# Second attention: a new order of units and banks, and score banks handed over one by one

## The reference, cut to what matters

```python
h = x                                      # [4, 512, 128]
q, k, v = h @ Wq, h @ Wk, h @ Wv           # 16 heads of 8 channels
q, k = rope(q), rope(k)                    # the angle depends on the sequence's number alone
s = (q @ k.T) * 8 ** -0.5                  # per sequence and head: 512 x 512, no mask
x = layernorm(x + softmax(s) @ v)          # this x is also kept: the final stage adds it again
```

## Time and profile before

| | us |
|---|---|
| three runs, median (lowest to highest) | 1745.11 (1740.25 to 1749.67) |
| the profiled execution | 1740.4 |
| its span, first to last instruction | 1737.5 |
| mean granted TensorE clock | 0.946 of full speed |

### The profile page before, as it was taken

One profiled execution on the slowest core, in us unless ns is written; L12 is line 12 of the kernel. 1 busy time (PEld: TensorE's weight loads), 2 busy tenths in 40 slices (PEclk: granted clock), 3 DMA queues, 4 the chain that ended last, 5 costly groups with the idle time before them and its releaser, 6 DMA issues. The chain is left out here.

```text
span 1737.5 us, 30440 instructions
## 1 busy us (share of the span) xinstructions
PE 1533.2 (88%) x10286; PEld 1045.5 (60%) x10286; DVE 1139.0 (66%) x2214; ACT 1077.1 (62%) x2354; POOL 512.3 (29%) x474
## 2 busy tenths in 40 slices
PE   6999999999799999999788888868899877999975
PEld 4777777777578888888533232224666544666643
DVE  2666666766577777777666667746777543676735
ACT  2655555555478888888546666655777633777741
POOL 0222222222321212222100000016666413767611
PEclk9999999999889999999968899988999987999988
DMA  7000000000012221122000000000000000000000
GB/s 225 2 2 0 0 0 0 0 0 1 1 64 74 73 73 69 65 72 73 1 1 1 1 1 1 1 1 1 2 1 2 2 0 1 1 2 1 1 1 24
DMA packets 18976, 36.35 MB, mean 21 GB/s; under 512 B 5748, under 2 KB 10992, under 8 KB 16688
## 3 DMA queue, kind: packets, MB, share of 16 engines
q1 hardware_dynamic: 18880, 35.09, 6.0%
HBM read 33.91 MB, written 1.18 MB: 20 GB/s over the span
## 5 line engine op out<-in xcount | busy, mean ns | idle before, releaser
L968 DVE TENSOR_TENSOR m_hidp<-m_hid,m_hidp 128x512 fp32r<-128x512 f32 x256 | 179.7, 728 | 76.6 <-ACT m_hidp L890 75.7
L389 ACT ACTIVATE a_prob<-ps,a_negmax 128x512 f32<-128x512 f32 (+3 forms) x256 | 133.8, 525 | 143.9 <-DVE a_negmax L459 143.9
L895 ACT ACTIVATE m_hid<-ps,pre_w 128x512 f32<-128x512 f32 x256 | 175.2, 685 | 61.8 <-PE ps L1104 61.3
L1159 PE MATMUL ps<-m_hidp,m_w2p 128*128 128x512 f32 x768 | 190.6, 397 | 0.0
L1104 PE MATMUL ps<-m_xp,m_w1p 128*128 128x512 f32 x768 | 189.7, 396 | 0.0
L1331 ACT ACTIVATE c_sb_pT<-ps 128x1024 f32<-128x1024 f32 x128 | 130.3, 1024 | 89.8 <-PE ps L1512 88.4
L1389 DVE TENSOR_REDUCE c_sb_negmax<-ps 128x2 f32<-128x1024 f32 x128 | 153.9, 1220 | 40.1 <-PE ps L1496 39.8
L345 POOL TENSOR_TENSOR a_qk_r<-a_qk_c,a_qk_s 128x512 f32<-128x512 f32 x64 | 81.3, 1270 | 330.9 <-DVE a_qk_s L450 330.9
L1788 ACT ACTIVATE l_sb_prob<-ps,l_sb_negmax,l_sb_rn 128x192 f32<-128x192 f32 (+1 forms) x256 | 123.9, 494 | 77.5 <-DVE l_sb_negmax L1880 77.5
L1104 PEld LDWEIGHTS ps<-m_xp,m_w1p 128*128 128x128 f32 x768 | 145.5, 190 | 36.5 <-issue 3.0
L1159 PEld LDWEIGHTS ps<-m_hidp,m_w2p 128*128 128x128 f32 x768 | 144.3, 188 | 34.8 <-issue 0.3
(11 more groups left out here) (227 smaller groups left out, 3197.2 us busy)
## 6 DMA issues: line engine op xcount, KB each, us to landing
m_gate_all<-m_gates_d SPq DMA_DIRECT2D x16, 1024.0 KB, 4.6
pre_w<-w1T SPq DMA_DIRECT2D x14, 258.0 KB, 2.7
pre_w<-w2T SPq DMA_DIRECT2D x14, 256.0 KB, 2.8
pre_wqkv<-wqkv SPq DMA_DIRECT2D x2, 768.0 KB
keep_xT<-xT SPq DMA_DIRECT2D x1, 1024.0 KB, 6.8
keep_x<-x SPq DMA_DIRECT2D x1, 1024.0 KB, 5.9
out<-keep_x SPq DMA_DIRECT2D x4, 256.0 KB, 2.3
pre_m_w<-l_w SPq DMA_DIRECT2D x2, 341.0 KB
```

Of the source, the lines that this page charges most:

```text
L389: nc.scalar.activation(prob[:, u % 4, 0:width(p)], score_ps(b, p, j)[:, 0:width(p)], ACT.Exp, bias=negmax[:, u:u + 1], accum_out=den[:, b ...
L895: nc.scalar.activation(hid[:, c % 2, f, :], ps[:, f, :], ACT.Gelu, bias=w1[:, k, FF + f:FF + f + 1]).then_inc(gelu_done, 1)
L968: nc.vector.tensor_tensor(hidp[:, c % 2, 1, f, :], hid[:, c % 2, f, :], hidp[:, c % 2, 0, f, :], ALU.subtract).then_inc(low_done, 1)
L1159: ins = nc.tensor.matmul(ps[:, 4 + c % 2, :], w2p[:, k, a, f, :], hidp[:, c % 2, b, f, :], start=(f == 0 and i == 0), stop=(f == FB - 1 an ...
```

## The change

Score units. TensorE waits for each bank of a pair by itself (`wait_bank`), every matmul of `max_scores` and every second matmul of `exp_scores` signals by itself, and `maxima` and `exps` are two instructions of one bank each, each with its own wait and signal. All counts that were in units are now in banks.

Banks. The turned maxima move from bank 7 to bank 6, which the sums use.

Order. TensorE's step r now has: r=0 to 3 `sums(m-1, r)`; r=2 also `turn_o(m-2)`; r=4 `project(m+3, 0)`; r=6 `turn_shift(m+1)`; r=7 `project(m+3, 1)`. The four `project_v` leave the lead-in and stand at r=0 to 3 of quad 0. In quad 15, three transposes of normalised sequences (`turn_x`) stand at r=3 to 5 and the first two `sums(15)` at r=6 and 7. On ScalarE `copy_o` is that of quad m-1, after unit 4, with `leading(m+3, 0)` behind it, and `leading(m+2, 1)` comes after unit 0. On VectorE `shift_remain` follows `shift_lead` directly, `remain(m+3, 0)` comes after unit k+6, and `remain(m+2, 1)` after k+1.

Normalisation. It is written into `attention1`. Sequences 0 to 2 are normalised while quad 15 is worked on, and VectorE makes their copies to `xT`; only sequence 3 is left for the end. GpSimd copies x for the final stage there, and the block `save_x` is gone.

```diff
-    shT_ps = m_ps.bitcast(BF16)[:, 0:S]
+    shT_ps = o_ps.bitcast(BF16)[:, 0:S]
...
-    def wait_pair(pe, turn):
+    def wait_bank(pe, turn, i):
...
         last = turn - 3
         if last < AHEAD:
-            pe.wait_ge(max_done, last + 1)
+            pe.wait_ge(max_done, 2 * last + i + 1)
...
         elif (last - AHEAD) % 2 == 0:
-            pe.wait_ge(exp_done, (last - AHEAD) // 2 + 1)
+            pe.wait_ge(exp_done, last - AHEAD + i + 1)
         else:
-            pe.wait_ge(max_done, (last - AHEAD - 1) // 2 + AHEAD + 1)
+            pe.wait_ge(max_done, last - AHEAD - 1 + 2 * AHEAD + i + 1)
...
@@ block.gpsimd
+        def save(b):
+            ts = slice(b * TPB, (b + 1) * TPB)
+            pool.wait_ge(norm_done, b + 1)
+            nc.gpsimd.tensor_copy(keep["x3"][:, ts, :], x[:, ts, :]).then_inc(kept, 1)
         for m in range(NQ):
+            if m == NQ - 1:
+                for b in range(LAST):
+                    deviation(b)
             values_in(m)
             if m >= 2:
                 add(m - 2)
+        for b in range(LAST):
+            save(b)
         add(NQ - 2)
         add(NQ - 1)
-        norm.pool(pool)
+        deviation(LAST)
+        save(LAST)
@@ block.scalar
         def exps(e):
             m, t, g = split(e)
-            act.wait_ge(e_mm, e + 1)
             if e % NUNIT == 0 and m >= 2:
                 act.wait_ge(pv_mm, m - 1)
-            nc.scalar.activation(pT[:, m % 2, g:g + 2, t, :], ps[:, pair(exp_turn(e)), :], ACT.Exp, scale=SCALE
-                                 ).then_inc(exp_done, 1)
+            for i in range(2):
+                act.wait_ge(e_mm, 2 * e + i + 1)
+                nc.scalar.activation(pT[:, m % 2, g + i, t, :], ps[:, pair(exp_turn(e)).start + i, :], ACT.Exp,
+                                     scale=SCALE).then_inc(exp_done, 1)
@@ block.vector
-            nc.vector.tensor_reduce(negmax[:, m % 2, i, g:g + 2], ps[:, pair(max_turn(k)), :], AX.X, ALU.max,
-                                    negate=True).then_inc(max_done, 1)
+            for i in range(2):
+                dve.wait_ge(max_mm, 2 * k + i + 1)
+                nc.vector.tensor_reduce(negmax[:, m % 2, t, g + i:g + i + 1], ps[:, pair(max_turn(k)).start + i, :],
+                                        AX.X, ALU.max, negate=True).then_inc(max_done, 1)
...
+        for b in range(LAST):
+            moments(b)
+        normalise(NQ - 3)
+        for b in range(LAST):
+            standard(b)
+            if b:
+                low_half(b - 1)
+                high_half(b - 1)
+        low_half(LAST - 1)
+        high_half(LAST - 1)
         normalise(NQ - 2)
         normalise(NQ - 1)
-        norm.vector(dve)
+        moments(LAST)
+        standard(LAST)
+        high_half(LAST)
@@ block.tensor
         def turn_shift(m):
             pe.wait_ge(sh_step, 2 * (m + 1))
-            pe.wait_ge(st_done, min(2 * (m + 3), 2 * NQ))
-            if m >= 3:
-                pe.wait_ge(att_done, m - 2)
+            if m == 0:
+                pe.wait_ge(st_done, 2)
+            elif m == 1:
+                pe.wait_ge(v_ev, NB)
+            else:
+                pe.wait_ge(oT_ev, m - 1)
...
         def sums(m, t):
             if t == 0:
                 pe.wait_ge(v1_done, m + 1)
+                pe.wait_ge(sh_ev, min(m + 2, NQ))
                 if m:
                     pe.wait_ge(oT_ev, m)
-                pe.wait_ge(exp_done, NUNIT * (m + 1))
+            pe.wait_ge(exp_done, 2 * (NUNIT * m + 2 * (t + 1)))
...
                 if e + AHEAD < ALL:
                     max_scores(e + AHEAD)
-                if r == 0 and m + 3 < NQ:
-                    project(m + 3, 0)
+                if m == 0 and r < NB:
+                    project_v(r)
+                if m and r < TPB:
+                    sums(m - 1, r)
                 if r == 2 and m >= 2:
                     turn_o(m - 2)
                 if r == 4 and m + 3 < NQ:
-                    project(m + 3, 1)
+                    project(m + 3, 0)
                 if r == 6 and m + 1 < NQ:
                     turn_shift(m + 1)
-                if r % 2 and m:
-                    sums(m - 1, r // 2)
+                if r == 7 and m + 3 < NQ:
+                    project(m + 3, 1)
+                if m == NQ - 1 and 3 <= r < 6:
+                    turn_x(r - 3)
+                if m == NQ - 1 and r > 5:
+                    sums(m, r - 6)
         turn_o(NQ - 2)
-        for t in range(TPB):
-            sums(NQ - 1, t)
+        sums(NQ - 1, 2)
+        sums(NQ - 1, 3)
         turn_o(NQ - 1)
-        norm.tensor(pe)
+        turn_x(LAST)
```

More of the change, by code:

```diff
@@ L1229, in attention1 @@
     x_add = sem("x_add")
+    n_const = sem("n_const")
+    stats_done = sem("stats_done")
+    mv_done = sem("mv_done")
+    var_done = sem("var_done")
+    rstd_done = sem("rstd_done")
+    norm_done = sem("norm_done")
+    n_mm = sem("n_mm")
+    low_ev = sem("low_ev")
+    high_ev = sem("high_ev")
+    kept = sem("kept")
     NQ = NB * QUADS
@@ L1234, in attention1 @@
     SCALE = HD1 ** -0.5
-    norm = Norm(nc, ctx, keep, ps, [0, 1, 2, 3], x_add, [QUADS * (b + 1) for b in range(NB)], "cn_", shifted=True)
+    LAST = NB - 1
     block = ctx.enter_context(nc.Block())
@@ L1353, in _ @@
             exps(e)
-            if m >= 2:
-                copy_o(m - 2)
+            if m == 0:
+                copy_v(0)
+            elif m + 2 < NQ:
+                leading(m + 2, 1)
             exps(e + 1)
+            if m == 0:
+                copy_v(1)
+            exps(e + 2)
+            if m == 0:
+                copy_v(2)
+            exps(e + 3)
+            if m == 0:
+                copy_v(3)
+            exps(e + 4)
+            if m:
+                copy_o(m - 1)
             if m + 3 < NQ:
                 leading(m + 3, 0)
-            exps(e + 2)
-            exps(e + 3)
-            exps(e + 4)
             exps(e + 5)
-            if m + 3 < NQ:
-                leading(m + 3, 1)
             exps(e + 6)
@@ L1433, in _ @@
             maxima(k)
-        for m in range(NQ):
+        for m in range(NQ - 1):
             k = m * NUNIT + AHEAD
[L1436 to L1440, removed]
+            maxima(k)
+            maxima(k + 1)
+            if m and m + 2 < NQ:
+                remain(m + 2, 1)
+            maxima(k + 2)
+            maxima(k + 3)
+            if m >= 2:
+                normalise(m - 2)
+            maxima(k + 4)
+            shift_lead(m + 1)
+            shift_remain(m + 1)
+            if m + 2 < NQ:
+                maxima(k + 5)
+                maxima(k + 6)
             if m + 3 < NQ:
                 remain(m + 3, 0)
[L1443 to L1459, removed]
-                maxima(k + 7)
+            if m + 2 < NQ:
+                maxima(k + 7)
+        for b in range(LAST):
[8 more added lines that the diff above has]
+        high_half(LAST - 1)
         normalise(NQ - 2)
         normalise(NQ - 1)
-        norm.vector(dve)
+        moments(LAST)
+        standard(LAST)
+        high_half(LAST)
     @block.tensor
@@ L1492, in max_scores @@
                 pe.wait_ge(st_done, 2 * (m + 1))
[L1493 removed]
             for g in (g0, g0 + 1):
                 r = slice(32 * g, 32 * g + 32)
[L1496 to L1498 removed]
+                wait_bank(pe, u, g - g0)
+                nc.tensor.matmul(ps[:, pair(u).start + g - g0, :], st[r, 0, m % 4, i * P:(i + 1) * P],
+                                 st[r, 1, m % 4, :], start=True, stop=True).then_inc(max_mm, 1)
         def exp_scores(e):
@@ L1546, in turn_o, with turn_x @@
             ins.then_inc(oT_mm, 1)
+        def turn_x(b):
+            pe.wait_ge(norm_done, b + 1)
+            if b == LAST:
+                pe.wait_ge(att_done, NQ)
+            elif b:
+                pe.wait_ge(high_ev, b)
+            else:
+                pe.wait_ge(att_done, NQ - 2)
+            for t in range(TPB):
+                ins = nc.tensor.transpose(m_ps[:, t * P:(t + 1) * P], x[:, b * TPB + t, :], ident[:, :])
+            ins.then_inc(n_mm, 1)
         project(0, 0)
@@ L1551, in _ @@
         max_scores(0)
-        project_v(0)
         max_scores(1)
@@ L1555, in _ @@
         max_scores(2)
-        project_v(1)
         max_scores(3)
@@ L1559, in _ @@
         max_scores(4)
-        project_v(2)
         max_scores(5)
@@ L1563, in _ @@
         max_scores(6)
-        project_v(3)
         max_scores(7)
@@ L2280, in _ @@
             turn_x2(NB - 1)
-def save_x(nc, ctx, keep):
-    saved = nc.alloc_semaphore("x3_saved")
-    block = ctx.enter_context(nc.Block())
-    @block.vector
-    def _(dve):
-        nc.vector.tensor_copy(keep["x3"][:, :, :], keep["x"][:, :, :]).then_inc(saved, 1)
 def finish(nc, ctx, keep, out):
@@ L2334, in program @@
                     xT_full=xT_full, xT=xT_full[:, :, 1:S + 1], pre=Preloaded(nc, ctx, io))
-        for phase in (attention0, experts0, attention1):
+        for phase in (attention0, experts0):
             run(phase, io, keep)
```

(2 more changed lines are left out.)

79 lines of the change are left out of this document (55 added, 24 removed).

## The result

The changed kernel takes 1727.39 us (median of 6 runs, 1725.0 to 1734.93), the kernel before 1742.89 on the same chips: a ratio of 0.9913, interval 0.9887 to 0.9938. It is faster by 15.5 us; the time lies inside the range of 1680 to 1730, but the gain is less than half of the 33 us forecast.

What follows compares the result with a forecast made beforehand. No engine was full: a full quad was 12.5 us of TensorE work at clock 0.91 plus 2.8 us of stalls. Savings of 22 + 0.7 + 5.5 + 5 = 33 us from 1740.4 gave 1707 us, range 1680 to 1730.

Steps and rivals of the forecast that it cites:

- One instruction per bank: Maxima and exponentials split by bank: VectorE +0.07 to +0.16 us a unit, ScalarE +0.08 to +0.18, lower ends taken.
- Walk of a full quad: Second attention, new order: 14.4 us a quad at full clock, 1.9 of it stalls, 0.9 less than before.
- the handover: Giving score banks over one by one: gain between -0.1 and +0.3 us, taken as 0.1 within the walk.
- Clock in the full quads: Eleven full quads: most dips go, clock 0.98, 14.7 us each instead of 16.74, 22 us saved.
- Lead-in and first quads: Start of the second attention, with four project_v moved to quad 0: 5.5 us saved together, bounds 1 and 12.
- The end from the last `copy_o`: From the second attention's last copy_o to local attention: 10.9 us instead of 18.1, 7.2 saved.
- Quads 13 to 15: Last quads of the second attention: 0.7 us saved in 13 and 14; quad 15 17.5 us against 15.6.
- The waits for VectorE in front of the turns of x: Quad 15: TensorE waits for VectorE's scaling and two copies between turns, two stalls of 1.4 us.
- the clock goes down: Rival, second attention: at clock 0.72 a quad takes 19.3 us, the whole is slower at 1768 us; chance 0.06.

Runs made afterwards that it cites:

- e3: The changed kernel with its new order, but maxima and exponentials again one instruction over both banks of a unit: 1745.93 us, ratio 1.0030 to the kernel before.
- e11: The changed kernel with turns of x after quad 15, unread wide products in quads 14 and 15, and 24 more in each of quads 2 to 13: 1708.50 us.
- e8: The kernel before, old order and two-bank instructions, with only normalisation written into the stage, turns of x after the last turn of outputs, no save_x: 1729.50 us, ratio 0.9924.
- e10: The changed kernel with each bank's first score product issued three times in steps 4 to 7 of quad 14 and all of quad 15: 1720.27 us, ratio 0.9905.
- e9: The changed kernel with turns of x after quad 15, unread wide products in quads 14 and 15, and max_scores products repeated at steps 6 and 7 of full quads: 1716.43 us.
- e5: The changed kernel with turns of x after quad 15, and 32-row score products repeated in quad 14's steps 4 to 7 and all quad 15: 1718.96 us, ratio 0.9877.
- e7: The changed kernel with turns of x after quad 15, unread wide products in quads 14 and 15, and eight at step 5 of quads 2 to 13: 1713.56 us.

## Why the prediction was wrong

- **One instruction per bank**: right. 1.29 and 1.08 us per unit, VectorE 12.1 us busy in a quad as computed. The two exponentials took 0.02 us less than my lower end.
  By the rule of the Trainium skill ("VectorE: DVE Perf Modes", "The TRN2 errata") I had estimated 1.32 us for the two reductions: near the 1.29 measured.
- **Walk of a full quad**: right. 14.4 us forecast, 14.57 measured at clock 1.00, with the stalls at the steps named (0.36, 0.44 and 0.71 us in the rows above, with some 0.5 more between the banks at r=6; forecast 0.4, 1.0 and 0.5). But I held the handover to be worth 0.1 us; e3 and the changed kernel show 0.43 us per quad in the new order.
- **Clock in the full quads**: mis-sized. Forecast 0.98 and 14.7 us, measured 0.95 and 15.24: 16.5 us saved instead of 22. I took it that shorter stalls would stop the dips. e11 shows that load does stop them; why eight products don't and 24 do stays open.
- **Lead-in and first quads**: 5.5 forecast, 6.2 measured (the lead-in 2.6 of them, where I had 3.5). **The end from the last `copy_o`**: 10.9 us forecast, 10.9 measured; e8 shows it worth 7.5.
- **Quads 13 to 15**: the step that failed. I forecast 0.7 saved in quads 13 and 14 and 1.9 lost in quad 15, with no term for the clock. The earlier trace rows had 1.00 for quads 13 and 14 of the kernel before, and I carried that over; for quad 15 the forecast names no clock at all. Measured: 4.8 and 14.1 lost, 17.7 us of the 22 missed. The change moves the sums to steps 0 to 3, so that little is left at steps 5 to 7 where there are no projections and, in quad 15, no maxima; I priced only the waits. Of the 17.7 us, the clock is at least 8.5 in quad 15 (e10) and 3.3 in quad 14 (16.4 us at clock 0.71, 13.1 at 1.00 in e11, which has more products in it). Quad 13 is another matter: forecast 12.9 us, measured 14.4 at 0.95, and still 14.0 at clock 1.00 in e9 and 14.55 in e11, so there the walk itself was too short. One more microsecond is a wrong reading: I set quad 15 against 15.6 us before, where its rows (1137.91 to 1154.4) give 16.5. The waits for VectorE in front of the turns of x I had counted as 2.8 us. They are 1.6 us in e10 at full clock (below), and 0.42 + 0.42 = 0.8 in the changed kernel, where slower products hide the rest.
TensorE's rows with waits for the copies of x, in e10:

```profile
1133.31 0.63 PE L1642 MATMUL ps<-keep_ident,keep_x 128*128 128x128 f32 x4 [0.74 <-DVE keep_xT L1484]
...
1135.90 0.63 PE L1642 MATMUL ps<-keep_ident,keep_x 128*128 128x128 f32 x4 [0.84 <-DVE keep_xT L1484]
```

- The rival "the clock goes down" had the mechanism, but I priced it with 28 us for the eleven full quads, where the clock rose instead, with 8 for quads 13 and 14 and with nothing for quad 15, and gave it 0.06. That the time still fell inside the range is in part luck: the range was wide for other reasons than this. The place where an order is thinnest is its last quads.

What stays open: what exactly holds the clock. e5 shows that narrow products do, in quad 15; e7 and e9 show that some extra work leaves dips as they are, or makes them rarer and longer. Nor is it shown why the old order holds 1.00 in quad 15 with more idle time.

## What to carry to other kernels

When an order packs TensorE's work together, list what each step holds in the last rounds of the loop too, where projections and look-ahead work have run out, and price those steps at the low clock. Two edits that each lose 0.3% can gain together (here with an end that both the new order and the whole change have): the finer handover paid here only in the order that has a wait for a handover on the path. Products that nobody reads can cost less than the low clock, here 3 us in eleven quads and 6 us in one by the traces. And try each part alone against the whole: here the new end by itself gave as much as all of it.

## What the runs showed of the hardware

TensorE's busy share did not tell its clock. Old quad 15: 81% busy with gaps of 1.64 us and 1.52 us, clock 1.00. New quad 15: 95% busy, clock 0.51 for 30 us, and 1.00 with repeated 32-row products in it (e10). The first of the old gaps:

```profile
1141.24 1.07 PE L1533 MATMUL ps<-c_sb_pT,c_sb_v 128*32 128x512 f32 x8 [1.64 <-ACT c_sb_oT L1338]
```

The low level itself makes TensorE look busy: a block of sums that takes 1.07 us here takes 1.94 in the new quad 15. So the busy column reads as full just where the engine is slowest.
